# Both cross attentions: turning and splitting the weights at the head of a step, mixing the values at its end

## The reference, cut to what matters

```python
q_r = ...                                   # queries, 16 heads, rotated and folded
kv_rope = kv_c * cos + rotate_half(kv_c) * sin        # kv_c: ctx, [32, 257, 128]
k_r = jnp.einsum('bld,hdr->bhlr', kv_rope, W_kr)
scores = jnp.einsum('bhsr,bhlr->bhsl', q_r, k_r)
attn = jax.nn.softmax(scores, axis=-1)
ctx_c = jnp.einsum('bhsl,bld->bhsd', attn, kv_rope)
ctx_lat = jnp.einsum('bhsd,hkd->bhsk', ctx_c, w_kc_kv)
out = ctx_lat.reshape(b, s, H * K) @ Wo.T
x = x + out
```

## Time and profile before

| | us |
|---|---|
| three runs of before | 2178.71, 2182.06, 2184.51 (median 2182.06) |
| the profiled execution, its own time | 2185.74 |
| its span | 2183.9 |
| L0x loop, from the first turned key to the last projection | about 128 to 417 |
| L1x loop, the same | about 1158 to 1454 |

### The profile page before, as it was taken

One profiled execution on the slowest core, in us unless ns is written; L12 is line 12 of the kernel. 1 busy time (PEld: TensorE's weight loads), 2 busy tenths in 40 slices (PEclk: granted clock), 3 DMA queues, 4 the chain that ended last, 5 costly groups with the idle time before them and its releaser, 6 DMA issues. The chain is left out here.

```text
span 2183.9 us, 27876 instructions
## 1 busy us (share of the span) xinstructions
PE 2045.7 (94%) x8746; PEld 1376.9 (63%) x8746; DVE 1146.7 (53%) x2682; ACT 798.0 (37%) x1986; POOL 974.1 (45%) x945
## 2 busy tenths in 40 slices
PE   7989999998899999999997999999986999999995
PEld 6856767676577854666664676757764555555552
DVE  4347878466442112455554788858864433444442
ACT  2344343143411100233334434334533444444441
POOL 1254664212274200477777466457302444555552
PEclk9999999999999999999998999999997999999998
DMA  5220001200211000011122000110045999988886
GB/s 192 103 69 22 27 23 42 79 2 1 97 58 39 29 18 0 27 41 53 41 86 68 21 27 23 69 66 1 24 150 172 294 299 323 228 216 216 209 213 165
DMA packets 83391, 209.19 MB, mean 96 GB/s; under 512 B 13728, under 2 KB 39840, under 8 KB 74752
## 3 DMA queue, kind: packets, MB, share of 16 engines
q1 hardware_dynamic: 60528, 153.54, 20.6%
q0 software_dynamic: 21280, 51.38, 11.4%
q10 hardware_dynamic: 1440, 2.49, 0.3%
HBM read 257.95 MB, written 34.36 MB: 134 GB/s over the span
## 5 line engine op out<-in xcount | busy, mean ns | idle before, releaser
L98 PE MATMUL banks<-L1f_w,L1f_xT 128*128 x760 | 263.8, 490 | 2.4 <-issue 1.2
L2662 POOL DMA_INDIRECT moe_sums<-L1f_y,L1f_row x95 | 150.7, 1586 | 220.6 <-DVE L1f_is_who L2531 165.1
L159 POOL TENSOR_TENSOR rstd<-rstd,power 128x1 f32<-128x1 f32 x48 | 29.2, 608 | 405.2 <-DVE rstd L153 405.2
L98 PEld LDWEIGHTS banks<-L1f_w,L1f_xT 128*128 128x128 f32 x760 | 137.7, 191 | 81.9 <-issue 6.7
L2670 POOL DMA_INDIRECT L1f_xg<-moe_rows,L1f_row x95 | 94.4, 993 | 63.2 <-DVE L1f_row L2526 36.4
L2498 DVE SCALAR_TENSOR_TENSOR L1f_z<-banks,L1f_share,L1f_sg 128x192 f32<-128x192 f32 x95 | 39.7, 418 | 145.8 <-ACT L1f_sg L2433 145.7
L461 PE MATMUL banks<-L0x_wn,L0x_qT 128*128 128x512 f32 x256 | 115.1, 593 | 0.8 <-DVE x L531 0.8
L461 PE MATMUL banks<-L1x_wn,L1x_qT 128*128 128x512 f32 x256 | 115.1, 593 | 0.8 <-DVE x L531 0.8
L98 PE MATMUL banks<-L0f_hT_hi,L0f_ug_hi 128*128 128x512 f32 x256 | 102.2, 399 | 11.4 <-POOL L0f_ug_lo L2061 8.7
L98 PE MATMUL banks<-L0f_down,L0f_z 128*128 128x512 f32 x256 | 111.1, 592 | 1.5 <-DVE L0f_z L1991 1.5
L2433 ACT ACTIVATE L1f_sg<-banks 128x192 f32<-128x192 f32 x95 | 31.5, 331 | 204.8 <-PE banks L98 204.8
(11 more groups left out here) (402 smaller groups left out, 5267.1 us busy)
## 6 DMA issues: line engine op xcount, KB each, us to landing
L1f_w<-in_experts SPq DMA_DIRECT2D x95, 1280.0 KB
L1f_laid<-moe_counts SPq DMA_DIRECT2D x59, 512.0 KB, 5.4
w<-in_L1x_heads SPq DMA_DIRECT2D x16, 704.0 KB, 4.0
w<-in_L0x_heads SPq DMA_DIRECT2D x8, 1216.0 KB, 5.3
w<-in_wug SPq DMA_DIRECT2D x8, 1024.0 KB, 4.7
L0x_craw<-in_ctx SPq DMA_DIRECT2D x96, 64.0 KB, 2.2
L1x_craw<-in_ctx SPq DMA_DIRECT2D x96, 64.0 KB, 2.0
w<-in_L0x_out SPq DMA_DIRECT2D x4, 1280.0 KB, 5.5
```

Of the source, the lines that this page charges most:

```text
L98: ins = pe.e.matmul(out, w, m, start=first and n == 0, stop=last and n == len(pairs) - 1)
L159: pool.e.tensor_tensor(self.rstd[:, i:i + 1], self.rstd[:, i:i + 1], self.power[:, 0:1], ALU.pow).then_inc(self.rstd_set.sem, 1)
L2662: pool.e.indirect_dma_start(self.sums[j % 2][:, :], bass.IndirectOffsetOnAxis(ap=self.row[:, j:j + 1], axis=0), self.y[j % self.NY][:], No ...
```

## The change

`LAG_VALUES` goes from 3 to 2, so that a batch's values are mixed in the same step in which its weights are turned. PE turns the weights first in a step and mixes last, after the projection. ACT rounds the weights first in a step. DVE moves the mixed values of batch b-3 (the same batch as before) and takes the rests first, and then does peak and weighing of batch b one behind the other. POOL splits before it rotates. The loops have 38 steps, projections begin in step 6, and `FIRST` becomes 10. No instruction is added or dropped and no shape changes.

```diff
-    LAG_TURN, LAG_VALUES = 2, 3
+    LAG_TURN, LAG_VALUES = 2, 2
...
     def pool_attention(self, pool):
         for b in range(B + self.LAG_VALUES + BPT):
-            if b + 2 < B:
-                self.rotate_keys(pool, b + 2)
             t = b - self.LAG_TURN
             if 0 <= t < B:
...
                 pool.e.tensor_tensor(lo[:], kv[:, 0:LC, :], hi[:], ALU.subtract).then_inc(self.kv_split.sem, 1)
+            if b + 2 < B:
+                self.rotate_keys(pool, b + 2)
...
     def tensor_attention(self, pe):
...
         for b in range(B + self.LAG_VALUES + BPT):
+            if 0 <= b - self.LAG_TURN < B:
+                self.turn_probs(pe, b - self.LAG_TURN)
             if b + 1 < B:
                 self.turn_keys(pe, b + 1)
             if b < B:
                 self.score(pe, b)
-            if 0 <= b - self.LAG_VALUES < B:
-                self.mix(pe, b - self.LAG_VALUES)
             if self.FIRST + b < XH:
                 pe.wait_ge(self.wn_set, self.FIRST + b)
                 self.fold_out(pe, self.FIRST + b, self.o_bank)
-            if 0 <= b - self.LAG_TURN < B:
-                self.turn_probs(pe, b - self.LAG_TURN)
             if b >= self.LAG_VALUES + BPT:
                 o = b - self.LAG_VALUES - BPT
                 self.project_out(pe, o // BPT, o % BPT)
...
+            if 0 <= b - self.LAG_VALUES < B:
+                self.mix(pe, b - self.LAG_VALUES)
...
     def mix(self, pe, b):
         if b == 0:
-            pe.wait_ge(self.wn_set, self.FIRST - 1)
+            pe.wait_ge(self.wn_set, self.FIRST)
...
     def scalar_attention(self, act):
...
         for b in range(B + self.LAG_VALUES + BPT):
+            t = b - self.LAG_TURN
+            if 0 <= t < B:
+                for c in range(LC):
+                    act.wait_ge(self.prob_turned, 2 * t + c + 1)
+                    act.wait_ge(self.mixed, t - 1)
+                    act.e.copy(self.pT[t % 2][0][:, c], self.t_bank[:, c * BANK:(c + 1) * BANK]).then_inc(self.pT_hi.sem, 1)
             if b + 1 < B:
                 self.keep_keys(act, b + 1)
             if b < B:
                 self.exponent(act, b)
             if self.FIRST + b < XH:
                 self.keep_folded(act, self.FIRST + b, self.o_bank)
-            t = b - self.LAG_TURN
-            if 0 <= t < B:
-                for c in range(LC):
...
     def vector_attention(self, dve):
         self.queries_done(dve)
         for b in range(B + self.LAG_VALUES + BPT):
-            if b < B:
-                self.find_peak(dve, b)
-            v, t = b - self.LAG_VALUES, b - self.LAG_TURN
+
+            v, t = b - self.LAG_VALUES - 1, b - self.LAG_TURN
             if 0 <= v < B:
...
             if b < B:
+                self.find_peak(dve, b)
                 self.weigh(dve, b)
```

More of the change, by code:

```diff
@@ L478, in scalar_attention @@
                 self.keep_folded(act, self.FIRST + b, self.o_bank)
-            t = b - self.LAG_TURN
-            if 0 <= t < B:
-                for c in range(LC):
-                    act.wait_ge(self.prob_turned, 2 * t + c + 1)
-                    act.wait_ge(self.mixed, t - 1)
-                    act.e.copy(self.pT[t % 2][0][:, c], self.t_bank[:, c * BANK:(c + 1) * BANK]).then_inc(self.pT_hi.sem, 1)
         self.after.halves_hi(act)
```

## The result

The changed kernel takes 2209.41 us (median of 4 runs, 2207.50 to 2210.84). The kernel before, on the same chip, takes 2181.93 (2178.71 to 2184.51). The ratio is 1.0117, with a 95% interval of 1.0105 to 1.0129: slower by 27 us. The forecast was 2211. The profiled execution of after took 2210.53 us, its span is 2208.7, against 2183.9 before.

What follows compares the result with a forecast made beforehand. PE was taken to set the pace at 8.26 us a step, DVE's chain close behind. Losses of 14.5 us in L0x and 15.4 in L1x, +29.9 on 2182.06, gave 2212, with 2211 taken; 8 in 10 from 2189 to 2227.

Steps and rivals of the forecast that it cites:

- What bounds before: Middle of L0x before the change: PE sets the pace at 8.26 us a step, DVE's chain close to it.
- the reading that DVE's chain bounded before already: Alternative reading of the kernel before: DVE's chain is already the bound, giving a loss of 27 to 40 us.
- DVE's step, 7.35 us: DVE's undisturbed step after the change: 5.04 plus move 1.14 and rests 1.21, less 0.04 overlap; 6.72 before.
- The disturbance, 4.3 us: POOL's burst slowing DVE per four steps: two weighings 3.4 us, small instructions 0.9 us.
- the upper bound: Upper bound on POOL's disturbance in four steps: 6.8 us, if all four weighings are hit.
- The cycle, 35.4 us: Four DVE steps in the middle, 31.1 us undisturbed plus 4.3; PE, needing 33.05, loses 2.3.
- The ramp: L0x start: step 0 5.3 us, later disturbed steps 8.85, first projection at 177.7, PE ends step 9 at 207.5.
- Middle and end: L0x steps 10 to 29 take five cycles, 177 us; last tile's first projection at 416.8, L0x losing 14.5.
- DVE fits: Rival: disturbance under 2.0 us in four steps, PE's pace holds, +1 us, 2183; chance 0.11.
- POOL falls in step with the mix: Rival: POOL waits for mixes in the middle, all four weighings hit, 37.1 us a cycle, +17 us, 2228; chance 0.07.
- A shorter ramp: Rival: POOL misses the ramp's weighings and the middle is quiet, -5.5 us a loop, 2171; chance 0.06.
- the sum of +29.9 us: Total forecast growth of both loops: L0x loses 14.5 us and L1x 15.4.

Runs made afterwards that it cites:

- light rotation: POOL's key rotation narrowed to 2 of 128 columns from batch 5 on: in the changed kernel 2166.67 us, in the kernel before 2174.81 us.
- the version with rests behind the peak: Changed kernel with DVE's step in the order move, peak, rests, weighing: 2178.0 us, ratio 0.9975 to the kernel before.
- the kernel with the transposes: Changed kernel with 20 extra identity transposes on PE ahead of each cross attention's first projection: 2205.26 us, ratio 1.0099 to the kernel before.
- POOL's order of before: Changed kernel with POOL rotating batch b+2 ahead of splitting batch b-2 again: 2228.78 us, ratio 1.02 to the kernel before.
- the peak first: Changed kernel with DVE taking the peak ahead of both move and rests: 2255.34 us, ratio 1.0315 to the kernel before.

## Why the prediction was right

*What bounds before.* PE's pitch of 8.26 with DVE just under it: shown from both sides. Take the disturbance away and before gains 8 us (light rotation), take the weighing away and it gains 15, in L0x both mostly in the ramp; lengthen DVE's step, as the change does, and PE waits. So the reading that DVE's chain bounded before already is wrong, although its price of 27 to 40 us holds the measured 27.

*DVE's step, 7.35 us.* Measured 7.20. The sum of pieces was too long by 0.15: less lay end to end than I took.

*The disturbance, 4.3 us.* Measured 4.05, with the two weighings at 2.88 and 2.85 (1.7 each, where 2.17 and 1.24 was taken), two L544 at 0.3 each, and no L549. The argument (the burst keeps its place in DVE's queue) held for the change's own order of POOL. The order of POOL's instructions, which I passed over, was worth 2.2 us a cycle: with before's order the disturbance would have been 6.3 (36.8 - 30.5), near the upper bound.

*The cycle, 35.4 us.* Measured 34.59. What PE loses, forecast at 2.3 us a cycle, is 34.59 - 33.05 = 1.5, of which the trace shows 1.3 as the wait (the prediction named 1.5 to 2.5).

*The ramp.* This step failed, at two places, and both made it too early. The fifth projection was due at 210.8 (PE ends step 9 at 207.5, and part 0 is 3.26 behind); it started at 217.62, 6.8 later. Step 0 was to be 5.3 since POOL was taken to be quiet. DVE's timeline of after:

```profile
131.87 1.53 DVE L541 TENSOR_REDUCE L0x_small<-banks 128x2 f32<-128x512 f32 x2 [12.37 <-PE banks L430]
...
136.59 2.56 DVE L554 TENSOR_SCALAR L0x_prob<-L0x_prob,L0x_small 128x256 f32<-128x256 f32 x4
139.07 1.28 DVE L541 TENSOR_REDUCE L0x_small<-banks 128x2 f32<-128x512 f32 x2
...
145.30 1.28 DVE L541 TENSOR_REDUCE L0x_small<-banks 128x2 f32<-128x512 f32 x2
...
149.62 2.90 DVE L554 TENSOR_SCALAR L0x_prob<-L0x_prob,L0x_small 128x256 f32<-128x256 f32 x4
...
154.58 1.27 DVE L541 TENSOR_REDUCE L0x_small<-banks 128x2 f32<-128x512 f32 x2
```

It is 139.07 - 131.87 = 7.20, because POOL was still at the rotation ahead of the split that waits. The steps with POOL beside them are 154.58 - 145.30 = 9.3, where 8.85 was taken: all four weighings were hit, as said, and the small instructions too. Together 3.8 us (the first projection at 181.54, not 177.7). The other 3.0 are the clock, which the sum did not have at all: 6.65 - 3.60.

*Middle and end.* By the prediction's own times the twenty-fifth projection is due at 387.7 (386.5 and the move). From the fifth on that is a forecast of +12.0 us for the middle and +7.2 for the end of L0x; measured are +7.5 and +4.2. Four cycles are 0.8 shorter than forecast and the first is 1.4 shorter: PE came late to the fifth projection, at 217.62, and DVE had ended the move for it at 215.75 + 1.16 = 216.91. The first wait in the middle came at the ninth, in step 14, as forecast. So the errors of the ramp (+6.8), the middle (-4.5) and the end (-3.1) nearly cancel: 13.7 against 14.5 in L0x. The sign and mechanism were right, and the closeness of 2211 to 2209 owes something to errors of opposite sign, which is luck. L1x has 11.3 against 15.4, so the sum of +29.9 us was 4.9 too high: the growth measured is 25.0.

*The rivals.* "DVE fits" would have needed under 2.0 us of disturbance in four steps; it was 4.05. "POOL falls in step with the mix" did not happen in the middle. "A shorter ramp" needed a quiet ramp and a quiet middle, and had neither: all four weighings of steps 2 to 5 were hit. The kernel with the light rotation has both, and took 2166.67 with PE busy 180.00 of 180, where the rival was priced at 2171; against before with the same light rotation that is 8 us, not 11.

*Busy shares.* The Trainium skill (Perfetto Trace Analysis, "Identifying the Most-Contended Engine") sets matmul share aside and names MFU, the share of the peak rate, and weight-load share in its place. In the middle of L0x weight loads are 123.69 of 180 us in before, and 126.42 in the version with rests behind the peak, where DVE waits for PE. Matmul share is 178.96 and 180.00. The constant pitch and DVE's waits for PE told the bound; neither of these two shares did.

## What to carry to other kernels

When two engines take turns in a ring, as peak, exponentials and weighing do here, put the work that needs neither between the halves. Taking it out made the ring longer than the pace of the engine that was to be helped, though no instruction was added. Where two engines disturb each other, move the disturbed operation to a third before reordering: the reordering moved 27 us one way or 5 the other, and with one operation moved to ACT every order tried was 12 to 15 us faster than before. And judge an order only in the queue orders it was made for, since one piece of a good order put alone into the other kernel cost 46 and 71 us.

## What the runs showed of the hardware

- POOL's work stretches some of DVE's instructions that have only SBUF on both sides: four multiplications of 128x256 from 1.14 to 2.9 us, an addition of 128x4 from 0.16 to 1.0, a sign change of 128x4 from 0.17 to 0.97. Not all: the reciprocal of 128x4, which stands between the addition and the multiplications, took 0.18 us each time, in the bursts too, in all runs. The ones that read PSUM took the same in the bursts and outside them: in the middle of L0x after the change the peak's reductions 1.27 to 1.28, the rests 1.27 to 1.29, the move 1.11 to 1.16. The Trainium skill (SBUF — State Buffer, "SBUF: two separate sides") gives the shared pair as an exclusive lock for a whole instruction, and an addition that grows by 0.84 while POOL's operations take up to 1.05 agrees. By the same section ScalarE never waits for that pair, and ACT's 1.71 us for four weighings in and out of the burst agree.
- PE's clock fell behind some short waits. After one of 3.14 us the projection took 6.65 us instead of 3.60, and the granted clock was 0.50 from 182 to 186 us, which is 1.2 GHz instead of 2.4 (1.00 in the kernel with the transposes). The length of the wait does not fix the price: in L1x of the same run it took 5.37 behind 3.13 us; with POOL's order of before, 5.37 behind 3.30 and 6.54 behind 3.29; with the peak first, mostly 5.37 behind 2.38, but once in each loop 3.67 behind 2.37. Behind 1.3 us it always took 3.67. So a wait of some 3 us cost 4.9 to 6.2 us in all.
